# Linear attention and gated experts on one core: 512-column products in two stages, and a new order of the stages around step 30

## The reference

```python
qkv = x @ Wqkv + bqkv; q, k, v = split(qkv)          # 256 columns each
q, k = q - mean(q), k - mean(k)
q2 = l2norm(q*q / (sum(q*q) + eps), axis=columns)
k2 = l2norm(k*k / (sum(k*k) + eps), axis=rows)
kv = k2.T @ v;  t2 = q2 @ kv / sqrt(1024)
x1 = layernorm(x + (v + t2) @ Wln + bln)
sel = sigmoid(x1 @ expert_sel.T)                     # 16 experts
scores = relu(x1 @ keys[e])                          # 256 -> 128, e = 0..15
ffn = sum over e of sel[e] * (scores[e] @ values[e]) # 128 -> 256
out = layernorm(x1 + ffn)
```

## Time and profile before

| | us |
|---|---|
| median of 3 runs | 1017.45 (1016.7 to 1018.49) |
| the profiled execution | 1022.25 |
| its span, first to last instruction | 1020.5 |
| TensorE busy | 997.0 (98%), 8324 matmuls |
| VectorE busy | 812.0 (80%) |
| ScalarE busy | 529.2 (52%) |
| GpSimd busy | 210.7 (21%) |
| DMA, share of the 16 engines | about 18% |

### The profile page before, as it was taken

One profiled execution on the slowest core, in us unless ns is written; L12 is line 12 of the kernel. 1 busy time (PEld: TensorE's weight loads), 2 busy tenths in 40 slices (PEclk: granted clock), 3 DMA queues, 4 the chain that ended last, 5 costly groups with the idle time before them and its releaser, 6 DMA issues.

```text
span 1020.5 us, 21965 instructions
## 1 busy us (share of the span) xinstructions
PE 997.0 (98%) x8324; PEld 984.7 (96%) x8324; DVE 812.0 (80%) x1874; ACT 529.2 (52%) x1150; POOL 210.7 (21%) x267
## 2 busy tenths in 40 slices
PE   7899999999999999999999999999999999999997
PEld 6789999999999999999999999999999999999997
DVE  4889887889768887798877888788887888778555
ACT  4566645566345653566445664456544566354323
POOL 0021112212222122221222112122211212122221
PEclk9999999999999999999999999999999999999999
DMA  5032111211122011220121311112111221111001
GB/s 184 22 113 75 44 43 62 88 62 43 43 99 90 22 44 63 84 94 32 44 73 54 105 43 43 63 54 94 43 43 62 83 66 43 43 65 42 23 2 42
DMA packets 47981, 62.19 MB, mean 61 GB/s; under 512 B 4098, under 2 KB 34562, under 8 KB 47876
## 3 DMA queue, kind: packets, MB, share of 16 engines
q1 hardware_dynamic: 47876, 60.79, 17.8%
HBM read 37.18 MB, written 23.07 MB: 59 GB/s over the span
## 4 chain that ended last, share of the span: by engine, by line
PE 85%; DVE 7%; ACT 3%; issue 2%; DMA 1%; SPq 0%; POOL 0%; DVEq 0%; ACTq 0%; POOLq 0%
PE up_bank L1333 31%; PE down_bank L1333 31%; PE ring_bank L1333 9%; PE qk_bank L1333 7%; PE g_bank L1333 3%; DVE x1T_l L959 1%; DVE gated_l L1103 1%; ACT z L642 1%; DVE gated L1097 1%; PE ring_bank L1584 1%; PE g_bank L1379 1%; PE ring_bank L1585 1%; ACT gated_h L560 1%; DVE qk L862 1%; DMA sel_rows<-sel 0%
## 5 line engine op out<-in xcount | busy, mean ns | idle before, releaser
L546 POOL PARTITION_BROADCAST sel_all<-sel_rows x240 | 196.1, 822 | 682.7 <-DVE gated L1097 615.7
L560 ACT ACTIVATE gated_h<-gated 128x512 fp32r<-128x512 f32 x256 | 161.5, 631 | 298.0 <-DVE gated L1097 294.4
L1333 PE MATMUL up_bank<-x1T_h,keys_h 128*128 128x256 f32 x1024 | 286.3, 280 | 2.1 <-DVE keys_l L1084 2.1
L1333 PE MATMUL down_bank<-vals_h,gated_h 128*128 128x256 f32 x1024 | 287.1, 280 | 0.3
L1333 PE MATMUL down_bank<-vals_l,gated_h 128*128 128x256 f32 x1024 | 286.2, 280 | 0.0
L1333 PE MATMUL down_bank<-vals_h,gated_l 128*128 128x256 f32 x1024 | 286.2, 280 | 0.0
L1333 PE MATMUL up_bank<-x1T_l,keys_h 128*128 128x256 f32 x1024 | 286.2, 279 | 0.0
L1333 PE MATMUL up_bank<-x1T_h,keys_l 128*128 128x256 f32 x1024 | 286.2, 279 | 0.0
L1103 DVE TENSOR_TENSOR gated_l<-gated,gated_h 128x512 fp32r<-128x512 f32 x256 | 172.2, 673 | 47.6 <-ACT gated_h L560 47.1
L1097 DVE SCALAR_TENSOR_TENSOR gated<-up_bank,sel_all 128x512 f32<-128x512 f32 x256 | 176.0, 688 | 39.5 <-PE up_bank L1333 34.9
L1333 PEld LDWEIGHTS up_bank<-x1T_h,keys_h 128*128 128x128 f32 x1024 | 194.0, 189 | 2.3 <-DVE keys_l L1084 2.3
(11 more groups left out here) (257 smaller groups left out, 1697.5 us busy)
## 6 DMA issues: line engine op xcount, KB each, us to landing
out<-z SPq DMA_DIRECT2D x32, 256.0 KB, 2.4
x_raw<-in_x SPq DMA_DIRECT2D x15, 512.0 KB, 4.8
xT_raw<-in_xT SPq DMA_DIRECT2D x14, 512.0 KB, 4.3
parked_q<-w_room SPq DMA_DIRECT2D x14, 512.0 KB, 2.6
q<-parked_q SPq DMA_DIRECT2D x56, 128.0 KB, 3.1
parked_x<-w_room SPq DMA_DIRECT2D x14, 512.0 KB, 2.6
w_room<-parked_x SPq DMA_DIRECT2D x56, 128.0 KB, 3.1
w_room<-in_keys SPq DMA_DIRECT2D x4, 512.0 KB, 4.5
```

The lines of the kernel that those rows point to most:

```text
L546: nc.gpsimd.partition_broadcast(sel_all[:, e % 2], row, P).then_inc(sel_spread, 1)
L560: return nc.scalar.activation(dst, src, ACT.Copy, **kw)
L1333: last = mm(dst, lhs, rhs, start=start and i == 0, stop=stop and i == n - 1, **kw)
```

## The change

- The QK stage is one product of 6 matmuls with 512 columns, where it was two of 6 with 256. The up product is so in steps 0, 3, 20, 21, 25 and 28 of each pass, and as before in the other 26.
- gT stands in the room of x_h and x_l, no longer in that of k2. The wait for the kv projection moves from the split of k2 to the first x split of a pass.
- QR 1 moves from step 27 to 25, XR 0 from 28 to 27, ZN 0 from 26 to 29, ZN 1 from 27 to 30, behind LG 0 in the plan of that step, and the bias of the third pair of x from 30 to 27.
- On SP's queue the gate rows of LG 0 stand behind the store of the first z of the group and ahead of the second; before, both stores stood ahead of them.

```diff
--- before.py
+++ after.py
@@ -45,12 +45,12 @@
         15: [("GG", 4), ("QK", 6), ("QS", 4)], 16: [("GG", 5), ("QS", 5)], 17: [("QK", 7)],
         18: [("ZA", 0), ("ZA", 1), ("QR", 0), ("GG", 6)], 19: [("KS", 0), ("GG", 7), ("QS", 6)], 20: [("KV", 0), ("QS", 7)],
         21: [("Y", 0)], 22: [("Y", 1), ("XS", 0)], 23: [("Y", 2), ("XS", 1)], 24: [("Y", 3), ("XS", 2)],
-        25: [("XS", 3)], 26: [("ZN", 0)], 27: [("QR", 1), ("ZN", 1)], 28: [("XR", 0)], 30: [("LG", 0)],
+        25: [("QR", 1), ("XS", 3)], 27: [("XR", 0)], 29: [("ZN", 0)], 30: [("LG", 0), ("ZN", 1)],
     },
 
 
     split_xT={4: 0, 9: 1}, split_x={5: 0, 10: 1, 13: 2, 16: 3},
-    bias_x={9: 0, 14: 1, 30: 2, 31: 3},
+    bias_x={9: 0, 14: 1, 27: 2, 31: 3},
 
     gpsimd_xT=(), gpsimd_x=())
 FIRST_PLAN = {
@@ -63,6 +63,7 @@
             gpsimd_xT=(), gpsimd_x=())
 LAST_STEPS = 3
 ROWS_STEP = 14
+WHOLE_UP = (0, 3, 20, 21, 25, 28)
 ROW_ROOMS = 3
 LAST_ROWS_STEP = 4
 BLOCK = 32
@@ -132,7 +133,6 @@
         wvl_h, wvl_l = sb("wvl_h", [P, M, C], F32R), sb("wvl_l", [P, M, C], F32R)
         kvw_h, kvw_l = sb("kvw_h", [P, M, C], F32R), sb("kvw_l", [P, M, C], F32R)
         k2_h, k2_l = sb("k2_h", [P, 2, C], F32R), sb("k2_l", [P, 2, C], F32R)
-        gT_h, gT_l = k2_h, k2_l
         ident, ones = sb("ident", [P, P]), sb("ones", [P, P])
 
 
@@ -141,6 +141,7 @@
         gated_h, gated_l = sb("gated_h", [P, HELD, GN], F32R), sb("gated_l", [P, HELD, GN], F32R)
         xT_h, xT_l = sb("xT_h", [P, G, M, GN], F32R), sb("xT_l", [P, G, M, GN], F32R)
         x_h, x_l = sb("x_h", [P, 2, C], F32R), sb("x_l", [P, 2, C], F32R)
+        gT_h, gT_l = x_h, x_l
         qT_h, qT_l = sb("qT_h", [P, 2, 2, M, P], F32R), sb("qT_l", [P, 2, 2, M, P], F32R)
         esel_h, esel_hl = sb("esel_h", [P, M, P], F32R), sb("esel_hl", [P, M, P], F32R)
         q2, x1 = sb("q2", [P, T, C]), sb("x1", [P, T, C])
@@ -576,6 +577,8 @@
                     at_least(act, x_in[i // 2], it * 16 + 16)
 
                     at_least(act, g_added, k_tile(it + 1, 2 * i - 1))
+                    if i == 0:
+                        at_least(act, kv_projected, it)
                     copy(x_h[:], x_raw[:, 2 * i:2 * i + 2]).then_inc(x_hi, 1)
 
             def squares(it, b, t):
@@ -601,7 +604,6 @@
                 act.wait_ge(k_scaled, n)
 
                 at_least(act, g_added, n - 2)
-                at_least(act, kv_projected, b - 1)
                 copy(k2_h[:, t % 2], k2[:, t % 2], scale=k_scale[:, t % 2:t % 2 + 1]).then_inc(k_hi, 1)
 
                 at_least(act, k4_summed, n - 1)
@@ -1514,13 +1516,9 @@
                         pe.wait_ge(xT_lo, k_half(b, h))
 
                         at_least(pe, qk_biased, k_tile(b, a) - 1)
-                        for half_of in range(2):
-                            cols = slice(half_of * C, (half_of + 1) * C)
-                            last = product(qk_bank[:, cols],
-                                           [(both(xT_h, xT_l, ALL, h, m, slice(i * P, (i + 1) * P)),
-                                             both(wqk_h, wqk_l, ALL, m, cols)) for m in range(M)],
-                                           start=half_of == 0, skip_group_check=True)
-                        last.then_inc(qk_projected, 1)
+                        product(qk_bank[:], [(both(xT_h, xT_l, ALL, h, m, slice(i * P, (i + 1) * P)),
+                                              both(wqk_h, wqk_l, ALL, m, ALL)) for m in range(M)],
+                                start=True).then_inc(qk_projected, 1)
                     elif kind == "GG":
                         pe.wait_ge(k_lo, k_tile(b, a))
                         pe.wait_ge(x_lo, k_pair(b, a // 2))
@@ -1596,13 +1594,18 @@
                         pe.wait_ge(piece_lo, 2 * (e // 4) + 1)
 
                     at_least(pe, gate_applied, f - 1)
-                    for half_of in range(2):
-                        cols = slice(half_of * QUARTER, (half_of + 1) * QUARTER)
-                        last = product(up_bank[s % 2][:, cols],
-                                       [(both(keys_h, keys_l, ALL, e, m, ALL),
-                                         both(x1T_h, x1T_l, ALL, g, m, cols)) for m in range(M)],
-                                       start=half_of == 0, skip_group_check=True)
-                    last.then_inc(up_made, 1)
+                    if s in WHOLE_UP:
+                        product(up_bank[s % 2][:], [(both(keys_h, keys_l, ALL, e, m, ALL),
+                                                     both(x1T_h, x1T_l, ALL, g, m, ALL)) for m in range(M)],
+                                start=True).then_inc(up_made, 1)
+                    else:
+                        for half_of in range(2):
+                            cols = slice(half_of * QUARTER, (half_of + 1) * QUARTER)
+                            last = product(up_bank[s % 2][:, cols],
+                                           [(both(keys_h, keys_l, ALL, e, m, ALL),
+                                             both(x1T_h, x1T_l, ALL, g, m, cols)) for m in range(M)],
+                                           start=half_of == 0, skip_group_check=True)
+                        last.then_inc(up_made, 1)
                 layer1(it, s)
                 if (it, s) == (0, 0):
                     queries0(3)
```

## The result

| kernel | median us | its profiled execution (span) us | 256-column matmuls at the quick pace | down product of step 0 behind the parking of x (mean of 7) |
|---|---|---|---|---|
| before | 1017.08 (1014.61 to 1018.49) | 1022.25 (1020.5) | 0.30 | 26.82 |
| changed | 1023.29 (1022.22 to 1024.15) | 1024.15 (1022.3) | 0.82 | 28.14 |

The changed kernel takes 1.0063 times the time of before, 95% interval 1.0041 to 1.0085. It is slower; the forecast was 1013.5 us and faster, and 1023.3 lies outside its range.

The account below looks back on a forecast made before the run. TensorE's stream and its few waits bound the kernel. Terms 0 - 7.4 + 3.5 = -3.9 us, taken from the median 1017.45, gave 1013.5 us; range 1005 to 1021.

Parts of the forecast that it names:

- Part 1: QK and six up stages: 624 pairs of 256-column matmuls become 512-column ones; taken as 0, ends -5.6 and +5.3 us.
- Part 2: TensorE's stream, steps 3 to 24: wide blocks raise the quick share from 0.27 to 0.69; net -7.4 us after new waits.
- Part 3: Moves around step 30: the logits' wait goes, but ZA and step 0's down product come later; about +3.5 us.
- Slower: the pace does not turn, and ZA is late: Rival on TensorE's stream and ZA: only the +3.5 us is left, 1021.0 us; chance 0.20.
- The moves are clean: Rival around step 30: ZN and the late sel copy fit VectorE's gaps, no new wait comes; 1005.8 us, chance 0.15.
- The fixed cost per instruction: Rival on TensorE: excess paid once per matmul, so 624 fewer save 6.2 us; with +3.5 it makes 1014.8; chance 0.10.
- end of part 3: Upper limit for the moves around step 30: +7 us, with ZA 0.5 later still.

Follow-up runs that it names:

- second trace: The changed kernel, unchanged, run again beside the kernel before, also rerun unchanged: 1023.80 us, ratio 1.0010; the rerun kernel before took 1023.84 us.
- all-wide kernel: Changed kernel with ZN back in steps 26 and 27 and all 32 up products in 512 columns instead of six: 1009.29 us, ratio 0.9910.
- ZN-back kernel: Changed kernel with the output normalisations back in steps 26 and 27, wide products and other moves kept: 1003.94 us, ratio 0.9857; in a later set 1001.78.

## Why the prediction was wrong, by its own steps

**Part 1, 512 columns: right.** Forecast 232.5 to 235 ns and no change; measured 232.6. The remark that it loses against a quick pair was in the bounds, and with a quick share of 0.8 this bound is the nearer one: 624 pairs at 5.9 ns where all is quick, 3.7 us.

**Part 2, the pace: the sum came out, its reason did not.** Forecast a quick share of 0.69 in steps 3 to 24 and -0.93 us a pass (7.4 over 8). Measured 0.82 over the whole stream and -1.6 us a pass outside the window in the six inner passes; ahead of the first window and behind the last the changed execution is 1.6 and 0.8 longer, so the whole is -7.3. That it meets the 7.4 is luck. The rule behind it, that every wide block turns a slow stream quick in 2 of 5 cases, was drawn from the logits, and for logits that don't wait it held or did better (in thirteen traces a slow stream turned quick at 19 of 34, and a quick one turned slow at none of 72). For the eight QK blocks, on which the forecast counted most, it failed: none of 72. The wide products alone take the share to 0.47; the moves alone take it to 0.63, since logits that need not wait leave a quick stream quick, while those that wait mostly leave a quick stream slow (13 of 16). Where the new wait at the down product of step 0 leaves the changed kernel slow (188.5, 801.4, 923.3), the wide up 3 behind it turns it quick within 3 us. The forecast counted no pace from step 25 to step 2 and so missed that the state at the end of this stretch is carried into the next pass.

**Part 3, the moves: this is the step that failed**, in the size of its sum: +3.5 forecast, 1.32 us a window, 9.2 in seven, measured. The chain was right down to the gate of 31 within 0.13 us (the table above). Two things were left out:
- From the gate of 31 to ZA the forecast had 6.4 us, as before; it took 6.9. The three gates are 2.41 and 2.49 apart instead of 2.20. For the second gap the row is VectorE's: gated_l is 0.97 us instead of 0.69, beside GpSimd's broadcast of the gate rows. In the kernel before, this broadcast starts 0.6 ahead of gated_l and costs it nothing; now the sel rows leave later, and it starts 0.2 ahead. For the first gap two paths are late by the same amount. One is VectorE's and ScalarE's: gated_h stands behind the sigmoid and starts 0.82 behind the gate of 31 instead of 0.71 (303.17), and gated_l then takes 0.81 instead of 0.69, again beside a broadcast. The other is the wait that the forecast did not have, that of the down product of step 30 for gated_l (5.4 us in all), which makes the next up product late. The chain of waits of the pass parked at 282.37 goes this way, from the end of gated_l of step 30 (301.56) on:

```profile
301.62 1.65 PE down_bank L1335 x12
303.27 1.49 PE up_bank L1335 x12
304.76 0.70 DVE gated L1099
```

  In the second trace the chain goes by gated_l in all seven passes, and the gap is 2.40 or 2.41 just the same; so the up product adds nothing to it. With both gaps, the clean window is 27.70, not 27.3: 0.4 a pass, 2.8 in all.
- The landing. XR in 27 leaves x1T_h at the mercy of the transfer: ScalarE waits for it in every pass, 14.7 us in all. The forecast took one landing (7.6 behind the parking); over seven passes it is 7.54 to 8.73, and in the second trace up to 9.57. A late landing makes the window late by as much, 0.44 on average, 3.1 in all. In the kernel before x1T_h started at 11.12 in every pass, which covered all of it. The spread stood in the trace of before: there the last of the four transfers lands 7.5 to 9.2 behind the parking, 8.0 on average over the seven passes. The forecast read one pass of them.

The two together are 5.9 us, and 9.2 less 3.5 is 5.7.

**The sum.** On the profiled executions the change came to +1.9 us (1024.15 against 1022.25) where -3.9 was forecast: part 3 is +5.7 over its forecast, and the six inner passes are some 2 below part 2's. Against that stand 1.6 us in the first pass, whose parking is at 159.96 instead of 158.38, and 0.8 behind the last window. In the second traces the first parking is at 158.26 in the changed kernel and 159.55 before, so the 1.6 belongs to the execution and not to the change.

**The base.** The forecast took this difference from the median. The profiled execution of before lay 4.8 above the median and in the upper half of its own spread (1012.7 to 1026.8), and the changed kernel, whose window is set by a chain, lies only 0.9 from its profiled time. That adds 4 us, and makes a difference that is nearly nothing in one set of runs 0.6% in another. That a gain which counts on a slow pace is worth less in quicker executions would explain it and is not shown: what share an execution of 1013 us has is open, since both traces of the kernel before, at 1022.25 and 1023.03 us, show 0.30.

**The rivals.** "Slower: the pace does not turn, and ZA is late", 1021, has the right sign with half of the mechanism: ZA is late and the pace did turn. The point from which it decides was given as a quick share of 0.43, with a price of 3.5; at the true price of 9.2 the share would have to be over 0.27 + 9.2 / 22.4 = 0.68 just to cancel. "The moves are clean" describes the window with ZN left where it was (1003.9 and 1001.8 us), not the change. It was argued away with the right row, the 1.31 us before sel that is a wait for ScalarE and grows. The fixed cost per instruction is refuted by the all-wide kernel. What was not priced at all was the change without ZN's move, and with it the size of the gain that ZN's move gives away: 19 us, of which the window is 2.4 us in seven passes, 17 together.

**The bound that was too narrow.** The end of part 3 was +7 and the measured value 9.2. It was drawn from 0.5 more on ZA; the landings in the trace of before, 7.5 to 9.2 behind the parking, allowed more.

## What to carry to other kernels

A step that feeds a chain with no slack should be moved by asking what it pushes on both engines it uses: here one normalisation costs VectorE 1.1 us and, through the z outputs on ScalarE ahead of the sel copy, another 1.0, in every pass. An early start that hangs on a transfer's landing takes on the whole spread of the landing, so price it with all the landings in the trace, not with one. A rate drawn from one kind of place (here logits) is a guess for another (here QK) until a row of that place shows it. And when a change has several edits, price the change without each of them: the best kernel here is the change less one edit.

## What the hardware showed beyond the forecast

- **Two paces at one granted clock.** The stream of 256-column matmuls runs at 113.3 or 117.8 ns with the clock at its full level (2.4 GHz) in both. It keeps its pace until a break, mostly. The share of the quick one went from 0.30 to 0.92 over these kernels by order and width alone. In the last of them, with its some 6750 matmuls of 256 columns, that is an estimated 6750 x 0.62 x 4.5 ns = 19 us, and TensorE is busy 977.6 us instead of 997.0. 512-column matmuls show one value at either, 232.5 in quick QK blocks and 232.2 in slow ones. What sets the pace behind a break is not settled: the traces give tendencies (behind a wide up 21 mostly quick; behind unwaited logits, met slow, quick in about half; behind waiting logits, met quick, mostly slow; behind wide QK, met slow, slow each time; behind the column sums of step 19 slow, whatever it was ahead of them), not a rule: one pass of the ZN-back kernel stayed slow through nearly all its wide blocks, from 253.7 to 380.2.
- **VectorE beside GpSimd.** The low half of the gate, which reads two tensors of SBUF, takes 0.69 us behind a wait and 0.81 or 0.97 (at 303.81 and 306.15) shortly behind the start of a broadcast. Of GpSimd's rows in time order (the second broadcast of the second row starts at 305.91):

```profile
303.42 0.80 POOL L547 PARTITION_BROADCAST sel_all<-sel  x1 [7.76 <-ACT sel L629]
305.25 1.46 POOL L547 PARTITION_BROADCAST sel_all<-sel_rows  x2 [1.04 <-DMA sel_rows<-sel]
```

Both end 1.20 to 1.21 behind the start of their broadcast. So do all 28 low halves in the two traces of the changed kernel that start 0.20 to 0.40 behind one: as if each stood still until 0.51 behind the broadcast's start and then took its 0.69. Those that start 0.60 or more behind take 0.69 although the broadcast is recorded as 0.80 long; a few that start 0.56 behind take 0.78, which this does not cover.

The Trainium skill, SBUF — State Buffer, section "🔬 SBUF: two separate sides", says that an instruction of VectorE with two SBUF inputs and one of GpSimd that reads SBUF lock the shared ports against each other for the whole instruction. The traces agree in form, since the low half is held up to a fixed point and does not share. They do not agree with a lock as long as the recorded broadcast: held until 306.71, a gated_l of 306.15 would end at 307.4, and it ends at 307.12. Whether the lock is shorter or the record of GpSimd too long is open.

- **The clock behind a wait.** A wait of 2.15 us for z was followed by the lower level of the granted clock (0.64 over 437 to 441 us) in the kernel with ZN 1 ahead of the logits, as were two more of its seven waits of 2.13 to 2.33 us; the other four, and the waits of 1.1 us at the same place in the changed kernel, were not.
- **The landing.** x1T_h, which waits for the parking of the room and the four transfers back, starts 7.4 to 9.7 us behind the start of the parking in the kernels that move it to step 27, with the same commands in every pass.
